# First cross attention of a two-layer decoder: score products over 64 of 128 rows, keys in one unpadded copy

## The reference

```python
q = (x @ Wq).reshape(b, n, 32, 16)
k, v = jnp.split(ctx @ Wkv, 2, axis=-1)          # 32 heads of 16 each
q = apply_axial_rope(q, pos_map)
k = apply_axial_rope(k, ctx_pos_map)
logits = jnp.einsum('bqhd,bkhd->bhqk', q, k) / np.sqrt(16)
w = jax.nn.softmax(logits, axis=-1)
attn = jnp.einsum('bhqk,bkhd->bqhd', w, v).reshape(b, n, 512)
return attn @ Wout + bout
...
x = _layernorm(x + _L0_xattn_ref(x, ctx_1024, fside_BxSx2_0, fside_BxSx2_0, ...))
```

## Time and profile before

| | us |
|---|---|
| median of three runs (3571.34 to 3575.84) | 3574.78 |
| the profiled execution, its own time | 3574.41 |
| its span | 3572.6 |
| PE busy (81% of the span) | 2898.9 |
| DVE busy (59%) | 2107.8 |
| ACT busy (50%) | 1787.9 |
| POOL busy (39%) | 1404.3 |
| four groups of the stage: POOL L873, DVE L1143, ACT L832, ACT L1064 | 293.3, 170.0, 159.6, 155.9 |

### The profile page before, as it was taken

One profiled execution on the slowest core, in us unless ns is written; L12 is line 12 of the kernel. 1 busy time (PEld: TensorE's weight loads), 2 busy tenths in 40 slices (PEclk: granted clock), 3 DMA queues, 4 the chain that ended last, 5 costly groups with the idle time before them and its releaser, 6 DMA issues. The chain is left out here.

```text
span 3572.6 us, 64599 instructions
## 1 busy us (share of the span) xinstructions
PE 2898.9 (81%) x24890; PEld 2048.9 (57%) x24890; DVE 2107.8 (59%) x4526; ACT 1787.9 (50%) x3852; POOL 1404.3 (39%) x1539
## 2 busy tenths in 40 slices
PE   3899989884888883899999778865999999952786
PEld 2566655552566662777777666654666676631332
DVE  4666666665677775454455455655555555556886
ACT  3444444443788885233222256644444444445775
POOL 1333333332788883345444424440121112112553
PEclk9988898996999996999999989987999999985998
DMA  4000000001000003000000000003000000030001
GB/s 166 7 7 7 7 7 1 7 7 63 1 2 2 2 2 131 20 7 7 7 7 13 25 10 2 2 24 131 7 7 7 7 7 7 7 138 22 1 1 48
DMA packets 35031, 83.08 MB, mean 23 GB/s; under 512 B 5283, under 2 KB 9381, under 8 KB 33574
## 3 DMA queue, kind: packets, MB, share of 16 engines
q1 hardware_dynamic: 34726, 78.95, 5.9%
HBM read 60.59 MB, written 4.19 MB: 18 GB/s over the span
## 5 line engine op out<-in xcount | busy, mean ns | idle before, releaser
L873 POOL TENSOR_TENSOR c_pT<-c_prob,c_pT 128x512 f16<-128x512 f32 x256 | 293.3, 1159 | 106.5 <-ACT c_pT L832 105.8
L1686 POOL TENSOR_TENSOR c_prob<-c_prob,c_inv 128x512 f32<-128x512 f32 x128 | 133.2, 1041 | 244.1 <-DVE c_inv L1880 244.1
L1064 ACT ACTIVATE c_prob<-psT 128x512 f32<-128x512 f32 x256 | 155.9, 609 | 69.9 <-PE psT L995 56.0
L873 POOL TENSOR_TENSOR a_pT<-a_prob,a_pT 128x384 f16<-128x384 f32 x128 | 117.8, 924 | 183.6 <-ACT a_pT L832 183.5
L1143 DVE TENSOR_REDUCE c_peak<-psS 128x2 f32<-128x512 f32 x256 | 170.0, 684 | 20.6 <-PE psS L976 17.2
L832 ACT CAST c_pT<-c_prob 128x512 f16<-128x512 f32 x256 | 159.6, 624 | 0.0
L345 POOL TENSOR_TENSOR a_q_rot<-a_q_cos,a_q_sin 128x512 f32<-128x512 f32 x64 | 81.1, 1267 | 196.3 <-DVE a_q_sin L590 196.3
L1820 ACT CAST c_pT<-psT 128x512 f16<-128x512 f32 x128 | 75.1, 586 | 153.2 <-PE psT L1698 153.2
L353 POOL TENSOR_TENSOR a_prob<-a_prob,a_inv 128x128 f32<-128x128 f32 x128 | 51.3, 401 | 254.6 <-DVE a_inv L622 254.6
L520 ACT ACTIVATE a_pT<-psT,a_kvh_t 128x256 f16<-128x256 f32 (+1 forms) x256 | 93.8, 418 | 104.1 <-PE psT L366 104.1
L1390 POOL TENSOR_TENSOR f_ch<-f_h,f_c 128x256 f32<-128x256 f32 x88 | 76.3, 867 | 147.3 <-DVE f_h L1581 147.3
(11 more groups left out here) (565 smaller groups left out, 11483.1 us busy)
## 6 DMA issues: line engine op xcount, KB each, us to landing
f_stage<-in_f_up_gateT SPq DMA_DIRECT2D x16, 352.0 KB, 7.9
c_stage<-in_L_xattn_Wq SPq DMA_DIRECT2D x10, 512.0 KB, 6.7
a_xcur<-x_all SPq DMA_DIRECT2D x9, 512.0 KB, 2.9
f_xcur<-x_all SPq DMA_DIRECT2D x9, 512.0 KB, 2.9
c_xcur<-x_all SPq DMA_DIRECT2D x9, 512.0 KB, 2.9
x_all<-in_x SPq DMA_DIRECT2D x1, 4096.0 KB, 13.9
a_stage<-in_L_attn_WqT SPq DMA_DIRECT2D x8, 512.0 KB, 7.5
a_stage<-in_L_attn_WoutT SPq DMA_DIRECT2D x8, 512.0 KB, 10.0
```

What stands on the lines that cost most here:

```text
L873: pool.tensor_tensor(pT[1][:, c % NPH, :], prob[:, c % NPX, :], pT[0][:, c % NPH, :], ALU.subtract)\
L1064: act.activation(prob[:, c % NPX, :], ST[c % 2][:, 0:EW], ACT.Exp).then_inc(s.e_done, 1)
L1686: pool.tensor_tensor(prob[:, h % NPB, :, :], prob[:, h % NPB, :, :], inv[:, h % NPB, :].rearrange("p (n a) -> p n a", a=1).broadcast_to([P ...
```

## The change

The padded copy of the keys goes. `kS` has one block for two heads (KB = 16 in place of 32), filled by one copy over 128 rows as `qS` is. The two clearings of `kS` on DVE at the start of the stage go too, and with them two counts of the semaphore `zeroed`, for which PE, ACT and DVE wait. Score products of a head now read 64 rows only, the half of the rows on which the head lies (`rows_of_head`). "S" goes from 18 to 19 and "peak" from 27 to 28: the head of `scores` and that of `scores_turned` in one turn now lie on opposite halves.

```diff
-    KH = H if HB > 1 else KVH
...
-        kS = sc.sb("kS", [P, 2, KH, N], F16)
+        kS = sc.sb("kS", [P, 2, KB, N], F16)
...
                 def k_of(h):
-                    return h if HB > 1 else h * KVH // H
+                    return h // HB if HB > 1 else h * KVH // H
+
+                def rows_of_head(h):
+                    return slice(h % HB * GD, (h % HB + 1) * GD) if HB > 1 else slice(0, P)
...
-                        last = pe.matmul(S[:, first:first + w], qS[:, b % 2, h // HB, n * P:(n + 1) * P],
-                                         kS[:, b % 2, k_of(h), 0:w], start=True, stop=not causal,
+                        last = pe.matmul(S[:, first:first + w], qS[rows, b % 2, h // HB, n * P:(n + 1) * P],
+                                         kS[rows, b % 2, k_of(h), 0:w], start=True, stop=not causal,
...
-                        last = pe.matmul(out, kS[:, b % 2, k_of(h), m * P:(m + 1) * P], qS[:, b % 2, h // HB, q0:N],
+                        last = pe.matmul(out, kS[rows, b % 2, k_of(h), m * P:(m + 1) * P], qS[rows, b % 2, h // HB, q0:N],
...
-                pe.wait_ge(s.zeroed, 7 if HB > 1 else 5)
+                pe.wait_ge(s.zeroed, 5)
...
-                if HB == 1:
-                    return copy(kS[:, b % 2, b0:b0 + nb, rows], src)
-                out = kS[:, b % 2, HB * b0:HB * (b0 + nb), rows].rearrange("p (j e) n -> p j e n", e=HB)
-                copy(out[0:GD, :, 0, :], src[0:GD])
-                return copy(out[GD:P, :, 1, :], src[GD:P])
+                return copy(kS[:, b % 2, b0:b0 + nb, rows], src)
...
-                if HB > 1:
-                    halves = kS[:, :, :, :].rearrange("p c (j e) n -> p c j e n", e=HB)
-                    dve.memset(halves[GD:P, :, :, 0, :], 0.0).then_inc(s.zeroed, 1)
-                    dve.memset(halves[0:GD, :, :, 1, :], 0.0).then_inc(s.zeroed, 1)
...
-                     "v0": 24, "v1": 26, "sk": [6, 8, 10, 11, 12, 13, 14, 15], "S": 18, "peak": 27, "PV": 5})
+                     "v0": 24, "v1": 26, "sk": [6, 8, 10, 11, 12, 13, 14, 15], "S": 19, "peak": 28, "PV": 5})
```

## The result

| | before | after |
|---|---|---|
| median of seven runs each, us | 3572.87 | 3587.19 |
| span of the profiled execution | 3572.6 | 3586.7 |

The ratio is 1.0040, with a 95% interval of 1.0028 to 1.0051: the changed kernel is 0.4% slower, by 14.3 us. 3571 had been forecast, 3.5 us faster; the time lies just inside the range given, 3557 to 3588, but it moved the other way.

The account below looks back on a forecast made before the run. No engine is full in the first cross attention; who is late in each part of the 32 steps matters. Seven batches at +0.4 give +2.8, the start -6.3: -3.5 from 3574.41, so 3571 us, range 3557 to 3588.

Parts of the forecast that it names:

- the price of the 64-row products: Score products in every step: changes of height cost only where PE is late and not waiting, +0.5 us a batch.
- The clock as a rival: PE idling ahead of the first query projection lowers the granted clock: 1.7 us a batch, 3583 us; chance 0.24.
- The shift: S 18 to 19, peak 27 to 28: +0.7 us at step 20 and +1.2 at steps 4 and 5, per batch.
- the late bank of x1: Steps 4 and 5: first query projection waits for the second transposed x's PSUM bank; +1.2 us a batch, bounds 0 and 2.1.
- The start and the copies: Stage start without DVE's clearing, -6.3 us once; one key copy in place of two on ACT, -2.0 us per batch.
- the bound of 1.55: Behind ACT's key copies POOL waits 1.55 us for ACT's cast; this could cap the copies' 2.0 us gain per batch.
- Halves that do not overlap: Rival on a step's score products: the four take 0.44 us, +4.6, with POOL's cap another +3.2; 3579 us; chance 0.14.
- The prediction's own middle value: A step's four score products: only second and third overlap, 0.33 us, between 0.22 and 0.44; step 0.83 us.
- The distance of the batches: First cross attention, from batch to batch: about 61.5 us; forecast wrong if it leaves 60 to 62.5.

Follow-up runs that it names:

- the added 64-row product: 128-row kernel of unpadded keys with the old table, plus one unread 64-row, 8-column product in each step: 3567.75 us; without that product 3552.06.
- The added products: One unread 128-row, 128-column product more per step: 128 rows, old table 3554.39 us; 64 rows, old table 3598.83; changed kernel 3586.28; 128 rows, new table 3571.16.
- the padded kernel: Kernel before with only both score products changed, to the head's own 64 rows out of the padded keys; copies, clearing and table stay: 3648.38 us.

## Why the prediction was wrong

**The step that failed** is the price of the 64-row products: "Elsewhere PE waits and the changes of height hide in that", +0.5 us per batch and +3.5 in all. Measured were 15.5, with the new table. Without them the change would have come out at -1.2. What the term rested on was right or too pessimistic: 0.1 us for a change of height (the added 64-row product shows 0.2 for two), and an overlap that was taken as half and is complete, so that a step is 0.72 and not 0.83. The mistake was to count only where PE sets the end by its own work. The forecast left the granted clock at its old value, and it is not the same with the new products: 0.86 in the ring, against 0.95 with 128 rows and the same table. With 64 rows every batch is slow at the value projections, on which the ring waits; with 128 rows and the same table two of seven are.

**The clock as a rival** named a mechanism that the traces bear out, and the wrong place. I put it in the wait ahead of the first query projection, with 1.7 us a batch, 3583. In the batch shown the time is lost at the value projections, at head 18 and at heads 1 and 2, with 4.3 us together, and in the last batch PE is at half clock for 27.3 us at a stretch. That 3583 came nearer to the measured time than 3571 is luck. In the price of the shift alone no part of the clock can be seen: the ring's is 0.92, and was 0.93, and heads 24 to 27 add nothing in sum. On top of the copies it has some: the ring's falls from 0.99 to 0.95, and two value projections at half clock cost 4.2 us there.

**The shift** had its chain, the late bank of x1, and its sum alone (13.3 forecast, 13.4 measured), but the sum is luck. The bank costs 17.0 us over seven batches in the trace and not 7 x 1.2 = 8.4, more than its bound of 2.1 a batch, and gains elsewhere that were not foreseen cancel the rest. Beside the single copies the shift costs 19.2: in the traces the bank's part is the same there, 16.8, the 4.2 of the clock come to it, and part of the gains falls away. That the costs of parts don't add was not in the sum.

**The start and the copies** were right in sum: -20.3 forecast, -20.4 measured. The start's 6.3 came as forecast, 4.7 of them at the first product. The copies' -14.0 were partly luck: ACT lost its 2.0 us of work per batch, but where the copies stand the ring lost only 1.2 to 1.3, less than the bound of 1.55, and what was missing came from value projections that now run at full clock.

**Halves that do not overlap** is refuted by the rows at 1060.55. The prediction's own middle value, that only the second and the third product can overlap because of their order, is refuted by them too. In the experiments with both heads on one half there is no overlap, a step is 0.93 us, and those are the ones in which the 64 rows cost most (24.5 and 74.8 us).

**The distance of the batches** was named as the test, 61.5 us and wrong outside 60 to 62.5. It came out at 62.4 to 65.3.

**What stays open** is why the clock stays low for so long with the 64-row products, up to 34 us with PE busy, and why it falls between two waits between which it stayed up. The added products show that two changes of height can bring a fall, and that more work shortens the time in none of the four kernels. Whether it is the height itself or what lies between the products was not told apart. How the 15.5 us divide between the clock, the changes of height and what a slower PE delays has not been shown either: the places agree, but no run held the clock fixed.

## What to carry to other kernels

A product's own time is not its price: here a step became 0.02 us shorter, and with 128 rows the same kernel was 15.5 us faster, so when products change in shape, read the granted clock of each stretch around a wait again, and ask which projection would run there at half speed. A sum that agrees proves none of its terms: two of the three here agreed by errors that cancelled, which only the distances place by place show. Where two banks serve all pieces in turn, a piece that stands one step ahead of another one's need was late in either order; moving x1 by one step gained more (6.7 us on the kernel before) than the whole change was to give. A wait that covers an engine's setup should stand only with the engine that uses it: the clearing held the first product back by 4.7 us without being needed there, and taking the wait away gave 3.8.

## What the runs showed of the hardware

Products on the two halves of the rows overlap completely, and the one issued third starts ahead of the one issued second: 1060.55 for both first products, 1060.66 and 1060.67 for the second ones. The Trainium skill, in "TensorE: Matmul & The Clock Gate", Part 3, gives such products a start some 4 ns apart; by that rule, the rows agree in size (0 and 10 ns). A change between 64 and 128 rows costs 0.1 us each way, in the changed kernel and with the added product (0.21 a step). Stretches at half clock inside the ring last 3.4 to 6.8 us where all products have 128 rows, and up to 34 us where the score products have 64 (34 us with 32.4 of PE busy, from 927 to 961 of the padded kernel). Where the ring ends and PE is idle in between, the kernel before has one of 20 us as well.
